# The high and low parts of a unit's made weight sums, and their store, one unit later than the sums

## The reference

```python
q_emb = relu(cond @ W3 + b3)                     # 64 x 512, the gate
v = relu(((64 * x + sum_over_rows(x)) * q_emb) @ W2 + b2)
w_up   = ((w_up_q - 7.5) * scale_up).T           # 512 x 2048, 4-bit codes, a scale for 64 of them
w_down = ((w_down_q - 7.5) * scale_down).T       # 2048 x 512
y1 = v @ w_up + b_up + v @ lora_up_a @ lora_up_b       # rank 16
x2 = relu(y1)
y2 = x2 @ w_down + b_down + x2 @ lora_down_a @ lora_down_b
out = x + y2
```

## Time and profile before

| | us |
|---|---|
| median of 3 runs | 748.3 (747.27 to 748.65) |
| the profiled execution | 747.43 |
| its span on the core | 745.5 |
| busy in the span: PE | 739.8 (99%) |
| DVE | 554.3 (74%) |
| ACT | 419.7 (56%) |
| POOL | 77.5 (10%), all in the first third |

### The profile page before, as it was taken

How to read it: one execution, slowest core, us unless ns; L and a number is a source line. 1 busy time by engine, 2 the same in 40 slices (tenths; PEclk the granted TensorE clock), 3 DMA queues, 4 the chain that set the end, 5 groups by cost and what they waited for, 6 DMA issues and landing times. The chain is left out here.

```text
span 745.5 us, 9634 instructions
## 1 busy us (share of the span) xinstructions
PE 739.8 (99%) x3274; PEld 612.8 (82%) x3274; DVE 554.3 (74%) x727; ACT 419.7 (56%) x727; POOL 77.5 (10%) x69
## 2 busy tenths in 40 slices
PE   9999999999999999999999999999999999999998
PEld 8888878878888888888888888888888888888886
DVE  6997866778948488677867697867775877757596
ACT  5963384766562565758556275666646353535540
POOL 0065533243420000000000000000000000000000
PEclk9999999999999999999999999999999999999999
DMA  9969979888464997655407896666516697555663
GB/s 293 323 177 341 337 231 285 260 254 277 157 208 144 376 340 223 215 190 191 158 29 255 291 377 221 224 198 197 184 58 195 223 382 226 190 191 191 194 196 128
DMA packets 92242, 170.21 MB, mean 228 GB/s; under 512 B 8418, under 2 KB 25186, under 8 KB 91682
## 3 DMA queue, kind: packets, MB, share of 16 engines
q1 hardware_dynamic: 91330, 168.20, 68.2%
q10 hardware_dynamic: 864, 1.39, 0.6%
HBM read 129.71 MB, written 40.89 MB: 229 GB/s over the span
## 5 line engine op out<-in xcount | busy, mean ns | idle before, releaser
L1187 PE MATMUL ps<-x_hi,ring 128*128 128x512 f32 x672 | 261.7, 389 | 0.2
L1188 PE MATMUL ps<-x_lo,ring 128*128 128x512 f32 x672 | 261.5, 389 | 0.0
L1189 PE MATMUL ps<-x_hi,ring 128*128 128x512 f32 x672 | 261.4, 389 | 0.0
L1187 PEld LDWEIGHTS ps<-x_hi,ring 128*128 128x128 f32 x672 | 126.1, 188 | 27.4 <-ACT ps L527 1.0
L1189 PEld LDWEIGHTS ps<-x_hi,ring 128*128 128x128 f32 x672 | 126.1, 188 | 26.2
L1188 PEld LDWEIGHTS ps<-x_lo,ring 128*128 128x128 f32 x672 | 126.1, 188 | 26.0
L410 ACT ACTIVATE xt<-xt,gated,gate_n 128x64 f32<-128x64 f32 x216 | 74.6, 431 | 34.8 <-DVE gated L781 34.8
L519 ACT ACTIVATE f<-ps,small_in 128x512 f32<-128x512 f32 x96 | 64.8, 691 | 41.7 <-PE ps L1189 41.7
L972 DVE TENSOR_TENSOR x_lo<-x_sum,x_hi 128x512 fp32r<-128x512 f32 (+1 forms) x96 | 76.7, 818 | 4.2 <-ACT x_hi L557 3.4
L893 DVE TENSOR_TENSOR ps<-s,ps 128x512 f32<-128x512 f32 x48 | 33.3, 693 | 49.6 <-PE ps L1189 49.3
L930 DVE TENSOR_TENSOR res<-ps,res 128x512 f32<-128x512 f32 x71 | 47.6, 687 | 20.1 <-PE ps L1189 19.8
(11 more groups left out here) (90 smaller groups left out, 1020.5 us busy)
## 6 DMA issues: line engine op xcount, KB each, us to landing
ring<-made_w SPq DMA_DIRECT2D x336, 256.0 KB, 3.8
made_w<-made SPq DMA_DIRECT2D x16, 1280.0 KB, 6.0
xt<-in_x SPq DMA_DIRECT2D x32, 256.0 KB, 6.2
code<-in_codes SPq DMA_DIRECT2D x16, 512.0 KB, 8.5
scale<-made_s SPq DMA_DIRECT2D x16, 512.0 KB, 8.1
made_w<-plain SPq DMA_DIRECT2D x64, 128.0 KB, 6.3
res<-in_x SPq DMA_DIRECT2D x4, 2048.0 KB, 10.2
out<-res SPq DMA_DIRECT2D x12, 512.0 KB, 5.4
```

The costliest lines, as they stand in the source:

```text
L1187: pe.matmul(dest, w_hi, a_hi, start=start, stop=False, skip_group_check=True)
L1188: pe.matmul(dest, w_hi, a_lo, start=False, stop=False, skip_group_check=True)
L1189: return pe.matmul(dest, w_lo, a_hi, start=False, stop=stop, skip_group_check=True)
```

## The change

`made_high(u)`, `made_low(u)` and `store_made(u)` are called one turn of the loop later, at the place where those of unit u + 1 stood. The three calls of units 13, 14 and 15 then stand together on ACT and on DVE, and SP has two stores at its loop's end. POOL's sums are where they were. Buffers, sizes and instructions are the same.

```diff
@@ SP, the loop over u
                 store_plain(u)
                 if 2 <= u < 10:
                     load_x(1, u - 2)
-                store_made(u)
+                if u > 0:
+                    store_made(u - 1)
+            store_made(UNITS - 1)
@@ ACT, u == 14
                     plain_high(15)
+                    made_high(13)
                     made_high(14)
                     made_high(15)
@@ ACT, u < 14
-                    made_high(u)
+                    if u > 0:
+                        made_high(u - 1)
@@ DVE, u == 14
                     plain_low(15)
+                    made_low(13)
                     made_low(14)
                     made_low(15)
@@ DVE, u < 14
                 if u < 14:
-                    made_low(u)
+                    if u > 0:
+                        made_low(u - 1)
                     add_lora(u + 2)
```

## The result

The changed kernel takes 784.38 us (median of 5 runs, 783.99 to 786.24) against 748.3 (747.27 to 749.68, 5 runs): 1.0491 times as long, 95% interval 1.0478 to 1.0504. The forecast was 781, range 762 to 803. The profiled execution has a span of 782.2 us against 745.5, 36.7 more.

The account below looks back on a forecast made before the run. TensorE was taken to bound the kernel (10.9 us a unit) until a 14.4 us one-unit ring held it. 28.8 to unit 13, 2.8 and 1.3 at the end make 32.9 us on 747.43, said as 781, range 762 to 803.

Parts of the forecast that it names:

- The ring: Sync queue and GpSimd: sums(u), codes(u+3), plain stores, x load, store_made(u-1), landing, sums(u+1) close in one unit, 14.4 us against 10.9.
- the signs named for being wrong: Code fetches at 11 to 12 us, TensorE's waits on something other than plain weights, or a granted clock under full.
- Where it takes hold: Sync queue: the ring paces code fetches from 74.5, then eight turns of 14.4 with x and one without, to 203.5.
- a(2): a(u) is the time codes(u+3) are issued; a(2) was put at 74.5, behind store_made(0) at 60.27, 9.5 and sums 4.7.
- From the ring to TensorE: Plain store, cast and low part: TensorE starts unit u+2 at a(u) + 11.5, unit 13 at 215.0 instead of 186.18, +28.8 us.
- The end: End of the block, behind plain_low(15): late made parts delay a z tile's bank, +2.8 us, and the next block, +1.3.
- the second stall of 1.3: Next block's start: TensorE would wait for the bank DVE's last evacuation frees, at +24.6, costing +1.3 us.
- High and low parts at nothing: ACT and DVE: high and low parts one unit later gain at most the 1.4 us TensorE waits; counted 0.
- The clock: TensorE: expected full; rival, half clock, 840 us if all matmuls slow, ring absorbing some 14 a unit; chance 0.04 for over 10 us.
- The landing by the Trainium skill's: Made store's landing: 2.0 us plus bytes over 436 GB/s, 5.0 us for 1280 KB, ring 12.7; the trace's row was preferred.
- the room covers it: Rival, loop over units: unit 13 keeps its start if the ring is 11.1 us; 746 to 750 us, chance 0.06.
- Crowded DMA: Rival, made stores: each lands as the one at 60.27, 10.56 us, ring 18.3, 816 us; chance 0.06.

Follow-up runs that it names:

- the queue alone: Kernel before, with only store_made one unit later on the sync queue, high and low parts left in place: 774.04 us, 1.0336.
- longer sums: Third of GpSimd's four sum instructions made three times in a row, in either kernel: 751.07 us on the kernel before, 814.95 us on the changed kernel.
- the codes behind the store: Changed kernel, with the codes of unit u + 3 fetched behind store_made(u - 1) instead of ahead of it: 757.88 us, 1.0128.

## Why the prediction was right

The ring, which makes most of the sum, was right in its mechanism and in each of its terms. That the time came within 4 us of 781 owes something to errors that cancel, told below; and of the signs named for being wrong, two came: TensorE waited mostly on something other than plain weights (12.7 us at L1252 against 4.7), and its granted clock fell. By its own steps, against the profile after:

- **The ring**: 14.4 us expected, 14.41 measured. Its terms, expected and in the mean of eight: issues 3.3 and 3.17; issue to sums 6.7 and 6.77; sums 4.4 and 4.45. The runs with the queue alone, with longer sums, and with the codes behind the store each bear out that it is this ring.
- **Where it takes hold**: a(2) 74.5, measured 74.45; a(10) 189.7 and 189.75; a(11) 203.5 and 203.64. The first of them is right partly by luck: the first store was issued 1.1 us sooner than I took (59.18, not 60.27), and the sums behind it took 5.62 us and not 4.7.
- **From the ring to TensorE**: right in its sum, wrong in its step. I let the plain cast come 9.1 us after the codes; it comes 5.6 after:

```profile
195.34 1.05 ACT L472 CAST plain<-whole 128x1024 fp32r<-128x1024 f32 x1 [6.04 <-DMA made_w<-plain]
```

The plain stores land sooner than before (median 3.6 us against 6.3), with the last made store long landed when they are issued. Unit 13's first matmul is at 213.03, not 215.0. But TensorE then waits in the middle of the unit, which I had not seen, for `add_lora` to free the bank of the low-rank product (L1252); that stands on DVE behind the made low part, which waits for ACT, which waits for the gate:

```profile
200.53 2.77 ACT L412 ACTIVATE xt<-xt,gated,gate_n 128x64 f32<-128x64 f32 x8 [4.14 <-DVE gated L785]
203.20 1.26 ACT L476 CAST made<-made_sum 128x1280 fp32r<-128x1280 f32 x1
...
204.49 1.49 DVE L833 TENSOR_TENSOR made<-made_sum,made 128x1280 fp32r<-128x1280 f32 x1 [2.86 <-ACT made L476]
205.90 1.28 DVE L824 TENSOR_TENSOR whole<-whole,ps 128x512 f32<-128x512 f32 x2
```

The row of `add_lora` at 205.90 releases the low-rank product at 206.63, after a wait of 2.1 us, and the same happens at 220.21 (1.6 us) in unit 13. Unit 13 starts 2.0 us earlier than forecast and takes 2.2 us longer than the 11.39 of before (186.18 to 197.57), and the two cancel: `w_tiles` is 29.06 late, 28.8 expected. This was luck, not insight.
- **The end**: mis-sized, 4.1 expected and 7.62 measured. The sums of unit 15 and the third tile's bank come as the chain had it, but I left out that `x1_high` waits for DVE's first `x1` sum, which stands behind made_low(15), and the clock:

```profile
252.83 1.27 ACT L476 CAST made<-made_sum 128x1280 fp32r<-128x1280 f32 x1 [6.83 <-POOL made_sum L752]
...
255.53 1.22 DVE L870 TENSOR_TENSOR x_sum<-fz,x_sum 128x1024 f32<-128x1024 f32 x1
...
256.79 1.99 ACT L455 CAST x_hi<-x_sum 128x1024 fp32r<-128x1024 f32 x2 [2.69 <-DVE x_sum L870]
```

These 2.69 us make the wait 5.42 instead of 2.8; the nine or ten matmuls at half clock behind it add 2.0; the second stall of 1.3, at the next block's start, did not come, since the evacuations at 273.68 were done in time.
- **High and low parts at nothing**: the step "I count 0" is right that there is nothing to gain, but wrong as a price of these parts alone, since 10 of the 36 us are theirs, by the run with the queue alone. The sum was not hurt by it, since the first store's 59.18 and the end's three parts were priced under the store's move.
- **The clock**: "stays full" was wrong. It fell behind waits of 5.4, 3.3, 2.7 and 1.7 us and once behind two of 0.8, but not behind others of 2.1. In the loop no time was won by filling the waits, which agrees with the rival's working that the ring absorbs slow matmuls, but the filling had a cost of its own; at the end the half clock took 2 us.
- **The landing by the Trainium skill's "DMA: Bandwidth & Descriptors" (Anatomy of one DMA)**: its estimate of 5.0 us would have given some 15 us less; the page fits it to DMAs issued by GpSimd, and this store is issued by the sync engine. The store landed in 5.1 to 9.5 us (median 6.5), and issue to sums was 6.77 in the mean; the row was the better guide. This store is issued behind up to 1.3 MB.
- **Rivals**: that the room covers it needs a ring of 11.1 us; with 14.41 it was far off. Crowded DMA came to 9.5 at most, for single stores.

## What to carry to other kernels

A store that is moved later on an in-order queue takes on every wait of the issues it is moved behind; look for the rings this closes, count how many loop turns each spans, and compare its length with that many turns. An engine with 93.7 us of waits costs nothing while its ring has room, and sets the pace once the ring is a turn shorter: some 2.5 us more of sums a turn cost 2.8 us in all before the change and 30.6 after. If such a step has to be late, put the fetch that waits for the ring's last member behind it, which here gave back 26.5 of 36.1 us.

## What the runs showed of the hardware that was not expected

- A plain store lands in 3.6 us (median) in the changed kernel, while the same form took 6.3 in the kernel before and 6.5 in the kernel with the codes behind the store. In the two slow cases a made store of 1280 KB is issued 0.5 to 3 us ahead of the codes, in the fast one some 11 us ahead. That this sets the landing fits the numbers; no run varies it alone.
- GpSimd's sum of 128x256 takes 0.72 to 0.75 us in 27 of 48 rows of the changed kernel, 1.2 in 8 and 1.7 to 2.3 in 13, and the four instructions of a unit moved between 3.4 and 6.8 us with it. All slow rows ran beside work of DVE, but some fast ones did so too. Made three times in a row, one of them lengthened the sums by 2.4 to 2.7 us in the mean and not by the 1.6 expected. Why a given row is slow, no run here settles.
- TensorE's granted clock went to half in short stretches behind waits of 0.8 to 5.4 us, and not behind three others of 2.0 to 2.1. Idle matmuls brought it back to full but for 3.4 us, without any gain in time (786.35 us against 784.38).
